# Graph attention on one core: the values' sum written to four output quadrants in turn instead of one

## The reference, cut to what matters

```
x: 8192 x 256, adj: 8192 x 8192 int32 (0 or 1), inlayer2: 8192 x 256
h      = max(layernorm(x), 0)
f1, f2 = (inlayer2 @ W.T + b) @ w1 + b1,  (inlayer2 @ W.T + b) @ w2 + b2
logits = f1[:, None] + f2[None, :]
coefs  = softmax(leaky_relu(logits, 0.01) + (-1e9 where adj is 0), axis=-1)
out    = x + coefs @ h
```

## Time and profile before

| what | value |
|---|---|
| median of 3 runs | 1459.9 us (1458.99 to 1459.92) |
| the profiled execution's own time | 1460.01 us |
| its span in the trace | 1458.2 us |
| TensorE busy | 1414.1 us, 97% of the span |
| VectorE busy | 1286.4 us, 88% |
| ScalarE busy | 613.0 us, 42% |
| GpSimd busy | 252.8 us, 17% |
| matmuls of the values' sum | 128, from 84.9 to 119.8 us |

### The profile page before, as it was taken

How to read it: one execution, slowest core, us unless ns; L and a number is a source line. 1 busy time by engine, 2 the same in 40 slices (tenths; PEclk the granted TensorE clock), 3 DMA queues, 4 the chain that set the end, 5 groups by cost and what they waited for, 6 DMA issues and landing times.

```text
span 1458.2 us, 33394 instructions
## 1 busy us (share of the span) xinstructions
PE 1414.1 (97%) x12585; PEld 1248.4 (86%) x12585; DVE 1286.4 (88%) x1396; ACT 613.0 (42%) x722; POOL 252.8 (17%) x249
## 2 busy tenths in 40 slices
PE   7479999999999999999999999999999999999998
PEld 6358888888888888888888888888888888888887
DVE  5899998989898989989898989899898989898894
ACT  1794444444343444434343444444343434444430
POOL 0371111111011111111110111111011101111111
PEclk9789999999999999999999999999999999999999
DMA  9959999999999999999999999999999999999940
GB/s 293 295 117 197 229 231 232 234 231 212 210 215 207 213 209 214 210 209 215 209 211 208 215 209 212 211 214 209 210 214 209 210 207 218 209 210 212 211 106 8
DMA packets 110164, 302.36 MB, mean 207 GB/s; under 512 B 11716, under 2 KB 44612, under 8 KB 110148
## 3 DMA queue, kind: packets, MB, share of 16 engines
q1 hardware_dynamic: 100720, 291.68, 89.5%
q10 hardware_dynamic: 9428, 10.49, 2.4%
HBM read 293.73 MB, written 8.39 MB: 207 GB/s over the span
## 4 chain that ended last, share of the span: by engine, by line
PE 92%; ACT 2%; SPq 2%; DMA 2%; DVE 1%; issue 1%; POOL 0%; POOLq 0%; ACTq 0%; DVEq 0%
PE acc L892 61%; PE acc L894 30%; SPq L281 2%; ACT h_f L472 1%; DMA H<-in_x_dram 1%; DMA adj_sb<-in_adj_dram 1%; ACT o_room L472 1%; DVE wgt L706 0%; ACT H L478 0%; PE rp L864 0%; DVE stats L644 0%; DVE wgt L632 0%; ACT rp L451 0%; DVE H L690 0%; DVE mv L651 0%
## 5 line engine op out<-in xcount | busy, mean ns | idle before, releaser
L892 PE MATMUL acc<-H,wT 128*128 128x257 f16 x8192 | 1354.6, 273 | 19.1 <-DVE wT L716 19.1
L894 PE MATMUL acc<-H,wT 128*128 128x257 f16 x4096 | 1119.4, 273 | 0.0
L892 PEld LDWEIGHTS acc<-H,wT 128*128 128x128 bf16 x8192 | 801.6, 98 | 121.4 <-issue 21.3
L451 ACT ACTIVATE mask<-adj_sb 128x1024 bf16<-128x1024 int32 x504 | 520.0, 1054 | 552.9 <-DVE wgt L706 441.3
L716 DVE STREAM_TRANSPOSE wT<-wgt 128x1024 f32<-128x1024 f32 x512 | 633.7, 1238 | 132.9 <-PE acc L894 132.7
L706 DVE SCALAR_TENSOR_TENSOR wgt<-b_word,c_word,mask 128x1024 f32<-128x1024 f32 x504 | 627.9, 1257 | 0.0
L894 PEld LDWEIGHTS acc<-H,wT 128*128 128x128 f16 x4096 | 401.2, 98 | 50.2
L399 POOL TENSOR_TENSOR x_res<-o_room,x_res 128x256 f32<-128x256 f32 x64 | 66.4, 1037 | 1131.3 <-ACT o_room L458 1100.8
L458 ACT ACTIVATE o_room<-acc,r_den 128x256 f32<-128x256 f32 x64 | 30.3, 473 | 246.2 <-DVE r_den L735 246.2
L404 POOL TENSOR_TENSOR o_room<-o_room,x_res 128x256 f32<-128x256 f32 x64 | 81.0, 1265 | 5.3
L401 POOL TENSOR_SCALAR o_room<-h_mean,no_nb 128x256 f32<-128x256 f32 x64 | 62.1, 970 | 0.0
(11 more groups left out here) (88 smaller groups left out, 159.2 us busy)
## 6 DMA issues: line engine op xcount, KB each, us to landing
adj_sb<-in_adj_dram SPq DMA_DIRECT2D x508, 512.0 KB, 8.5
x_res<-in_x_dram SPq DMA_DIRECT2D x64, 128.0 KB, 4.0
out_dram<-o_room SPq DMA_DIRECT2D x64, 128.0 KB, 4.3
H<-in_x_dram ACTq DMA_DIRECT2D x16, 256.0 KB, 12.7
H<-in_x_dram SPq DMA_DIRECT2D x16, 256.0 KB, 13.6
wgt<-in_L_gnn_inlayer_dram ACTq DMA_DIRECT2D x8, 256.0 KB, 9.8
wgt<-in_L_gnn_inlayer_dram SPq DMA_DIRECT2D x8, 256.0 KB, 10.6
adj_sb<-in_L_gnn_inlayer_dram ACTq DMA_DIRECT2D x8, 256.0 KB, 12.5
```

Of the source, the lines that this page charges most:

```text
L451: nc.scalar.activation(place, adj_sb[:, c, g * CQ:(g + 1) * CQ], ACT.Relu, scale=M_SCALE).then_inc(m_ready, 1)
L892: pe.matmul(acc[:, par, 0:DV], w_hi[:, k % 4, t, :], H[:, j, part, 0:DV], start=(j == 0 and part == 0), stop=False)
L894: mm = pe.matmul(acc[:, par, 0:DV], w_lo[:, k % 4, t, :], H[:, j, 0, 0:DV], start=False, stop=(j == ROWS - 1))
```

## The change

The sum's matmuls write to four groups of PSUM partitions in turn, starting at partitions 0, 32, 64 and 96 by the slice number modulo 4 (Q is 4, B is 32), instead of all to partitions 0 and 1. Inside a strip the loops over part and slice change places, so that neighbouring matmuls go to different quadrants. As 120 of the 128 partitions are not written by them, VectorE zeroes the whole 128x256 area of PSUM once (`hs_zeroed`), after the four V operations that read the same PSUM bank. The copy into `h_sum` and the matmul of ones take all 128 partitions instead of 2. The wait for `D_parts_ready` is now in the first strip only, with a wait for `hs_zeroed` beside it.

```diff
-        h_sum = sb("h_sum", [2, D], F32)
+        h_sum = sb("h_sum", [P, D], F32)
...
-        hs_ps = small[0:2, 1, 0:D]
+        hs_ps = small[:, 1, 0:D]
...
+            dve.wait_ge(u_ready, Q)
+            nc.vector.memset(hs_ps, 0.0).then_inc(hs_zeroed, 1)
             dve.wait_ge(cst_ps_ready, 1)
             nc.vector.tensor_copy(cst[:, :], cst_ps).then_inc(u_ready, 1)
...
             def sum_of_values(k):
 
-                pe.wait_ge(D_parts_ready, 2)
-                for j in range(TS * k, TS * (k + 1)):
-                    for part in range(2):
-                        mm = pe.matmul(hs_ps, D_inv_parts[:, j, :], H[:, j, part, 0:D],
-                                       start=(j == 0 and part == 0), stop=(j == ROWS - 1 and part == 1))
+                if k == 0:
+                    pe.wait_ge(D_parts_ready, 2)
+                    pe.wait_ge(hs_zeroed, 1)
+                for part in range(2):
+                    for j in range(TS * k, TS * (k + 1)):
+                        a = B * (j % Q)
+                        mm = pe.matmul(hs_ps[a:a + 2, :], D_inv_parts[:, j, :], H[:, j, part, 0:D],
+                                       start=(j < Q and part == 0), stop=(j >= ROWS - Q and part == 1))
                 return mm
...
-                    pe.matmul(hm_ps, ones[0:2, :], h_sum[:, :], start=True, stop=True).then_inc(h_mean_ps_ready, 1)
+                    pe.matmul(hm_ps, ones[:, :], h_sum[:, :], start=True, stop=True).then_inc(h_mean_ps_ready, 1)
```

More of the change, by code:

```diff
@@ L198, in graph_attention @@
         zeroed = sem("zeroed")
+        hs_zeroed = sem("hs_zeroed")
         ident_ready = sem("ident_ready")
```

## The result

The changed kernel takes 1462.17 us (median of 17 runs, 1460.81 to 1464.26), the kernel before 1459.59 us beside it (median of 17). The ratio is 1.0017, with a 95% interval of 1.0010 to 1.0024: slower by 0.17%, within what I had called no change. The profiled execution took 1461.94 us.

A forecast was written before the change was run, and what follows sets the result against it. Bound: TensorE's pace from the second row tile on, its start set by VectorE's copy. From 1460.01 us: sums 0, MEMSET 0, copy and ones 0, clock +2.0 gives 1462.0, against the median 1461.9; range 1458.8 to 1463.6.

The forecast's parts named there:

- The bound: Second row tile on: TensorE's pace limits; its first product, at 121.59 us, moves the end microsecond for microsecond.
- The closed loop: TensorE's matmuls from the second row tile on run without a hole, 12096 times 0.110 = 1331 us.
- The sums: First row tile: a sum's 1.75 us falls to 0.44 with four quadrants overlapping, or stays at 1.75 without overlap.
- The gain of nothing by itself: First row tile: the 10.5 us saved on TensorE all become idle time before the copy; worth 0 us.
- The clock: Second row tile's start: granted clock falls in TensorE's wait of about 5.2 us, costing 2.0 us (1.3 to 2.7); chance 0.50.
- No fall: Rival, wait before the second row tile: clock stays up or sums do not overlap, nothing changes; 1459.9 us, chance 0.34.
- Changing quadrants costs: Rival, first row tile's sums: each quadrant change costs 0.09 us, a sum grows by 1.35; 1469 us, chance 0.09.
- An earlier copy: Rival, end of first row tile: VectorE reaches the copy earlier, at most 0.9 us gained; 1459.0 us, chance 0.07.
- Small parts: Zeroing in the prologue (0 to 0.6 us, covered), copy on 128 partitions, ones over 128 rows (0 to 0.1 more): 0.

The follow-up runs named there:

- e8: Changed kernel with VectorE's copy of the sum one step earlier, behind the second row tile's first turn and weights; 1459.35 us, ratio 0.9998.
- e5: Changed kernel with the matmul of ones moved behind the second row tile's third strip and VectorE's copy into h_mean moved later; 1460.30 us, ratio 1.0000.
- e9: Changed kernel with the late matmul of ones, plus ScalarE's first-row-tile scaling moved between the third row tile's two mask groups; 1456.81 us, ratio 0.9977.
- e1: Changed kernel with 44 more matmuls of no other purpose behind the last sum, filling TensorE's wait; 1459.34 us, ratio 0.9998.
- e2: Kernel before, one quadrant and no zeroing, with only 4 of the 16 matmuls of each sum; 1462.33 us, ratio 1.0018.
- e4: Changed kernel with 22 matmuls of no other purpose behind the last sum, filling half of TensorE's wait; 1460.67 us, ratio 1.0003.
- e7: Changed kernel with the sum's loops in the order of before (slice outside, part inside), so two neighbours share a quadrant; 1461.59 us, ratio 1.0014.
- e3: Changed kernel with all matmuls of the sum in the first quadrant, everything else kept; 1459.44 us, ratio 0.9997.

## Why the prediction was right

*The bound.* The closed loop and the place of the copy behind turn(1, 1) held to 0.05 us in the trace after. That this place is what holds TensorE was shown by moving it (e8) and by taking the wait away (e5, e9). One sentence on the bound was too strong: that a microsecond by which the second row tile's first product starts earlier moves the end by one. In e5 that product starts 5.2 us earlier than before the change, and the end is no earlier; in e9 4.9 us earlier, and the end comes 2.9 us earlier. (In their traces 0.8 and 0.5 us of this are the first row tile's own earlier start.) The turns and ScalarE's scaling come next. For a later start the sentence holds (1.9 us in the changed kernel's trace), and only that was asked of it here.

*The sums.* I had bounded a sum between a quarter and no gain. A strip takes 108.22 - 104.93 = 3.29 us against the 3.26 worked out with a quarter, and TensorE is through at 115.99 against 115.8. By these lengths the four quadrants overlap completely; a sum now costs 1.75 - 1.29 = 0.46 us, where a quarter is 0.44. The wait ahead of the second strip is 2.07 us instead of the 1.6 expected, since the clock rose at 84.0 us in this trace, 1.1 us earlier than before.

*The gain of nothing by itself.* Filled with useless work (e1), the changed kernel is where the kernel before is. Of the freed 8 x 1.29 = 10.3 us, 8.7 left TensorE's busy time ahead of the second row tile and became idle time; the rest went into matmuls at the low clock.

*The clock.* The mechanism was right: +2.0 predicted, +1.9 between the two profiled executions, +2.6 by the medians of 17. That the time came within 0.3 us of the forecast (1462.17 against 1461.9) is in part luck, as the price was 0.6 too low and the kernel before, at 1459.59, was 0.3 below the 1459.9 I started from. Where the 0.7 us between the medians and the traces comes from stays open. Behind the ones' wait the low clock lasted 4.0 us in the changed kernel's trace, and 2.9 to 3.6 in those of e2, e4, e7 and e8, all inside my 2.6 to 5.5; the runs up to 1464.26 might have had longer stretches, which no trace shows. The ones at the low clock (0.40 us) were not in my sum as a term of their own. I had given the fall a chance of 0.50 on the strength of two falls from 1.00 to 0.50, 4.1 us (46.85 to 50.99) and 3.2 us (61.41 to 64.64) into a wait. That a shorter time at the low clock before the restart means a shorter one behind it was my assumption. The traces since show falls 2.0 to 2.5 us after the last work, but also 5.0 and 5.2 us after it. All three traces with a wait of 5 us (changed kernel, e2, e7) have the low clock at the restart or within 0.3 us of it, so 0.50 was rather low; in how many executions it falls is not known, since each kernel has one trace.

*The rivals.* No fall: refuted by the trace, and by e1 against the changed kernel. Changing quadrants costs: refuted; a sum takes 0.61 us with 15 changes of quadrant and 0.62 with 7 (e7), so nothing is added for a change. An earlier copy: not seen, the trace has it 0.05 us later.

*Small parts.* Zeroing 0.27 us, inside the 0 to 0.6 and covered as said; the copy 0.39 us instead of 0.37; the ones 0.70 instead of 0.69 at full clock (e3).

## What to carry to other kernels

Before making an engine's work cheaper, find out what comes right behind it and in whose list that stands: here the freed time could only be had by moving one wait on TensorE and one operation on ScalarE, each an edit of a few lines. Ask of a shortened TensorE stage not only whether the gain is hidden but how long TensorE then idles: in these traces 13 of 21 waits of 1.97 to 5.05 us ended in a restart at a granted clock of 0.50, and where such a restart is on the path, as in the changed kernel, the shorter work makes the kernel slower (here by 2.6 us). A wait that a profile does not show may have only half a microsecond to spare; when a stage is moved forward, look up what each of its waits was released by, and when.

## What the runs showed that I had not expected

- How long TensorE idles before the clock falls varies widely, and the length of the wait does not settle it. In the ones' wait it fell 2.2 us after the last work in the changed kernel (115.99 to 118.17) and in e8 (116.31 to 118.52), 2.3 us in e4, and 5.0 and 5.2 us in e7 and e2; before the change the delays were 3.2 and 4.1 us. Ahead of the first row tile's second strip, waits of 1.97 (e8) to 2.40 us (e1) lost the clock in six traces, while one of 2.55 us (e4) kept it. Ahead of its fifth strip eight traces have a wait of 2.02 to 2.05 us, the changed kernel's among them: seven kept the clock, and e5 lost it at 101.28. Counted from 79 to 150 us in all traces with short sums, waits of 1.97 to 5.05 us lost the clock in 13 cases of 21, and waits up to 1.72 us in none.
- Sixteen matmuls of 256 columns over four quadrants take 0.75 us from product to product, whatever their order (e7: 0.76), against 2.04 us in one quadrant (108.79 to 110.83 before the change).
- The spread goes with the long wait, but not with it alone: 3.4 us between fastest and slowest with the wait (17 runs), 1.1 us with the wait filled (e1, 11 runs). Of the kernel before, 16 of the 17 runs lie within 1.1 us and one is at 1463.92; beside e1 to e4, four of its 33 are above 1462. What those few had no trace shows.
